# A four-layer network on one core: masked exponents in the state-space stage, its batch change rearranged, and three vector steps of the RWKV stage given to GpSimd

## The reference

```
# layer 0, the mix of each token with the one before it
xx   = shifted(x) - x
mix  = tanh((x + xx * maa_x) @ maa_w1.T)          # four low-rank mixes
xf_f = x + xx * (maa_f + delta_f)                 # f = receptance, decay, key, value inputs

# layer 3: 4 heads, state 128, 256 inner channels
z, x, B, C, dt, A, trap, angles = split(u @ W_in)
adt   = min(-softplus(A), -1e-4) * softplus(dt + bias);  ell = cumsum(adt)
theta = cumsum(angles * dt)
K, Q  = rope(rmsnorm(B) + B_bias, theta), rope(rmsnorm(C) + C_bias, theta)
S[i,j]= (Q_i . K_j) * exp(ell_i - ell_j) * step(i, j)      # zero for i < j
y     = (S @ x + D * x) * silu(z);  out = y @ W_out
```

## Time and profile before

| | |
|---|---|
| time, median of 3 | 2929.28 us (2923.33 to 2929.88) |
| profiled execution | 2918.22 us, of it 2916.0 us from the first to the last instruction |
| busy over the span | PE 2353.3, DVE 2163.2, ACT 1709.3, POOL 1020.3 us |
| granted TensorE clock, mean | 0.893 of full speed |
| RWKV pre stage | 44 to 334 us |
| state-space stage | 2573 to 2916 us, 8 batches |

### The profile page before, as it was taken

The page is one execution under the profiler, slowest core; times in us unless marked ns, Lnnn a source line. Parts: engine busy times, 40 slices in busy tenths (PEclk is TensorE's granted clock), DMA queues, the critical chain, the costliest instruction groups (busy, mean ns, idle before and its releaser), DMA issues. The chain is left out here.

```text
span 2916.0 us, 36851 instructions
## 1 busy us (share of the span) xinstructions
PE 2353.3 (81%) x10377; PEld 1041.9 (36%) x10472; DVE 2163.2 (74%) x5969; ACT 1709.3 (59%) x3093; POOL 1020.3 (35%) x987
## 2 busy tenths in 40 slices
PE   7666378786778999769999989778878888768887
PEld 2211267664343434333333333323331111234443
DVE  6999589995686665556666656587579999567777
ACT  4444344543655666562222278646579999677775
POOL 0222488994244555240000044200020000048886
PEclk8777666767889999989999999989889999889999
DMA  3112575625175765431111033200031111011110
GB/s 132 58 58 73 128 137 108 111 42 148 54 225 109 141 120 109 108 138 48 34 35 37 24 82 91 60 0 0 17 109 45 45 42 43 16 42 33 40 37 26
DMA packets 297801, 211.63 MB, mean 73 GB/s; under 512 B 157640, under 2 KB 262008, under 8 KB 296952
## 3 DMA queue, kind: packets, MB, share of 16 engines
q1 hardware_dynamic: 258992, 189.71, 24.6%
q0 software_dynamic: 20352, 17.05, 4.0%
q10 hardware_dynamic: 18256, 2.52, 0.5%
HBM read 136.18 MB, written 62.52 MB: 68 GB/s over the span
## 5 line engine op out<-in xcount | busy, mean ns | idle before, releaser
L3171 ACT ACTIVATE ca_pw<-ca_ps,ca_mx 128x512 f32<-128x512 f32 x512 | 342.7, 938 | 7.3 <-DVE ca_mx L3207 7.3
L3207 DVE TENSOR_REDUCE ca_mx<-ca_ps 128x1 f32<-128x512 f32 x512 | 311.2, 675 | 0.7 <-PE ca_ps L3138 0.7
L3004 DVE CUSTOM_DVE_ANT_0 mx_sums<-mx_ps,w_w2f 128x384 f32<-128x384 f32 (+3 forms) x512 | 218.0, 486 | 112.2 <-PE mx_ps L2959 110.7
L2947 PE MATMUL gm_ps<-gm_h,w_w2f 128*128 128x512 f32 x512 | 239.0, 607 | 3.1 <-DVE gm_h L3032 3.1
L3171 ACT ACTIVATION_READ_ACCUMULATOR ca_pw<-ca_ps,ca_mx 128x1 f32 x512 | 234.3, 458 | 0.0
L3138 PE MATMUL ca_ps<-qs,ks 128*128 128x512 bf16 x484 | 172.6, 397 | 60.3 <-ACT ca_pw L3171 41.0
L2646 ACT ACTIVATE ta_pw<-ta_ps,w_cst 128x1280 f32<-128x1280 f32 x128 | 168.1, 1322 | 36.2 <-PE ta_ps L2526 36.1
L3076 ACT ACTIVATE gm_h<-gm_ps,w_w2f 128x512 f32<-128x512 f32 x64 | 44.0, 687 | 218.4 <-PE gm_ps L2947 218.4
L2372 ACT ACTIVATE at_pw<-at_ps 128x1280 f32<-128x1280 f32 x128 | 157.1, 1238 | 20.8 <-PE at_ps L2339 20.8
L2778 DVE TENSOR_TENSOR ta_pw<-ta_pw,w_cst 128x384 f32<-128x384 f32 x128 | 70.7, 552 | 132.6 <-ACT ta_pw L2646 128.6
L2691 POOL DMA_INDIRECT Acc<-XN,f_idx x64 | 104.6, 1635 | 153.8 <-DVE XN L2749 139.1
(11 more groups left out here) (574 smaller groups left out, 6202.1 us busy)
## 6 DMA issues: line engine op xcount, KB each, us to landing
Pd<-s_p SPq DMA_DIRECT2D x48, 384.0 KB, 4.6
ex_w<-e_w SPq DMA_DIRECT2D x48, 256.0 KB
Qd<-rp_q SPq DMA_DIRECT2D x4, 2048.0 KB, 11.6
ss_ellb<-Rd SPq DMA_DIRECT2D x32, 256.0 KB, 3.3
qs<-Pd SPq DMA_DIRECT2D x32, 192.0 KB, 4.1
ks<-Pd SPq DMA_DIRECT2D x32, 192.0 KB, 4.5
Pd<-cs_p SPq DMA_DIRECT2D x16, 384.0 KB, 2.4
GX<-Qd SPq DMA_DIRECT2D x44, 128.0 KB
```

The lines of the kernel that those rows point to most:

```text
L2947: last = pe.matmul(at, W(("h1", "h2")[layer])[:, j * 512 + f * 128:j * 512 + (f + 1) * 128], (h0, h1)[layer][:, j, :], start=(j == 0), sto ...
L3004: return v.tensor_tensor_reduce(out=sums[:, bank, at:at + n], in0=ps[:, bank, at:at + n], in1=K["w2f"]("down")[:, T - n:T], scale=-1.0, sc ...
L3171: act.activation(pw[:, h % BUF, jk, :], ps[:, (h * NB + jk) % BANKS, :], ACT.Exp, bias=mx[:, h % H, jk:jk + 1], accum_out=z[:, h % H, jk:j ...
L3207: v.tensor_reduce(mx[:, h % H, jk:jk + 1], ps[:, q % BANKS, :], AX.X, ALU.max, negate=True).then_inc(S["top"], 1)
```

## The change

Three groups of edits.

State-space stage. (1) The decays of a diagonal block get their mask within the exponent: POOL's new `fallen` adds a constant block `later` (0 for a query not before the key, -1e30 otherwise) to ell, where DVE took the minimum before; `low` has a tile for each head now. (2) POOL's `steps` has two instructions a head: strict mask times (gamma - beta dt), a column that the rows stage now makes in COL[:, 0], and plus beta dt; the wait for `clamp` is gone. (3) The order at the change of batch: PE projects the first gate before keys and queries, spreads head 0 before `out`, and the dx products and the next batch's angle projection come between spread(1) and products(0); ACT does Sin, Abs and Sin between the gates and ahead of Ln and Exp, and its dummy Exp is gone; DVE makes bc first and rot after it under a semaphore of its own, `finish` comes behind prepare(0) and its addition at the end of the batch, `add_angles` comes before weigh(0), `one_turn` before weigh(3).

RWKV pre stage. (4) `differences` (without L147, which stays on DVE) and the fourth addition of L169 (the value input) are POOL's; the additions on DVE are three a lane. POOL makes the differences of the next iteration right behind the value inputs of this one. PE's value product and ACT's first Sigmoid wait for the new semaphore xv.

```diff
@@ rwkv_pre_phase, vector
-            def differences(i, a):
+            def shifted(i, a):
                 x = halves(i, a)
-                v.wait_ge(S["xf"][a], i)
-                v.tensor_tensor(xp[:, a, M:T], x[:, 0], x[:, 1], ALU.subtract)
-                v.tensor_tensor(xp[:, a, 1:M], x[:, 1, 0:M - 1], x[:, 0, 1:M], ALU.subtract)
-                v.tensor_scalar(xp[:, a, 0:1], XN[...], -1.0, None, ALU.mult).then_inc(S["diff"][a], 1)
                 v.wait_ge(S["diff"][a], i + 1)
...
-                    for f in range(4):
+                    for f in range(3):
                         last = v.tensor_tensor(split(xf[:, a, f, :]), split(t[:, a, f, :]), x, ALU.add)
@@ rwkv_pre_phase, gpsimd
+            def values_in(i, a):
+                t = buffers(i)[0]
+                g.wait_ge(S["f1"][a], 2 * i + 1)
+                g.wait_ge(S["vps"][a], i)
+                g.tensor_tensor(split(xf[:, a, 3, :]), split(t[:, a, 3, :]), halves(i, a), ALU.add).then_inc(S["xv"][a], 1)
+            for a in range(LANES):
+                differences(0, a)
             for i in range(IT):
+                for a in range(LANES):
+                    values_in(i, a)
+                if i + 1 < IT:
+                    for a in range(LANES):
+                        g.wait_ge(S["xxx"][a], i + 1)
+                        differences(i + 1, a)
@@ l2_gelu_and_rows_phase, vector
-            v.tensor_copy(COL[:, 0:3], cps[:]).then_inc(P["col"], 1)
+            v.tensor_copy(COL[:, 1:3], cps[:, 1:3]).then_inc(P["col"], 1)
...
+            v.tensor_tensor(COL[:, 0], COL[:, 1], COL[:, 2], ALU.subtract).then_inc(P["col"], 1)
@@ ssm_phase, tensor
+            def first_gate(i):
                 pe.wait_ge(S["at"], i + 1)
                 project(i, 7, W("in")[:, 0:128]).then_inc(S["z0"], 1)
+            def second_gate(i):
...
+                spread(0)
+                if i:
+                    out(i - 1)
+                spread(1)
+                pe.wait_ge(S["xt"], i + 1)
+                for n in range(2):
+                    pe.matmul(ps[:, 5 + n, :], dx[...], XN[...], start=True, stop=False, ...)
+                if i + 1 < B:
+                    angles(i + 1)
                 products(0)
...
                 products(3)
                 if i + 1 < B:
+                    first_gate(i + 1)
                     keys_and_queries(i + 1)
-                    gates(i + 1)
+                    second_gate(i + 1)
@@ ssm_phase, scalar
                 gate(i, 0)
+                act.wait_ge(S["clamp"], i + 1)
+                act.activation(th[:, 2, :], th[:, 0, :], ACT.Sin).then_inc(S["sin"], 1)
+                act.activation(th[:, 1, :], th[:, 0, :], ACT.Abs).then_inc(S["abs"], 1)
                 act.wait_ge(S["bcps"], i + 1)
                 act.activation(sq[:], ps[:, 3:5, :], ACT.Square).then_inc(S["sq"], 1)
                 gate(i, 1)
+                act.wait_ge(S["abs"], i + 1)
+                act.activation(th[:, 1, :], th[:, 1, :], ACT.Sin, scale=-1.0, bias=cst("halfpi")).then_inc(S["cos"], 1)
                 act.wait_ge(S["ms"], i + 1)
                 act.activation(sq[:], ps[:, 0:2, :], ACT.Ln, bias=cst("eps")).then_inc(S["std"], 1)
...
-                act.activation(table[:, i:i + 1], cst("eps"), ACT.Exp)
@@ ssm_phase, gpsimd
+            def fallen(i, h):
+                g.wait_ge(HD["ell"][h], 16 * (i + 1))
+                g.wait_ge(HD["dec"][h], i)
+                g.tensor_tensor(low[:, h], ellb[:, h, :].rearrange("p (j x) -> p j x", j=NB),
+                                cst("later").unsqueeze(1).to_broadcast([128, NB, 128]), ALU.add).then_inc(HD["low"][h], 1)
             def steps(i, h):
                 g.wait_ge(HD["dm"][h], i)
+                g.tensor_tensor(mm[:, h], cst("stri")..., COL[:, 0, :, ...]..., ALU.mult).then_inc(HD["m1"][h], 1)
                 g.wait_ge(HD["m1"][h], i + 1)
-                g.tensor_tensor(mm[:, h], mm[:, h], own[:], ALU.add).then_inc(HD["m2"][h], 1)
+                g.tensor_tensor(mm[:, h], mm[:, h], COL[:, 2, :, ...]..., ALU.add).then_inc(HD["m2"][h], 1)
...
-                g.wait_ge(S["clamp"], i + 1)
+                for h in range(H):
+                    fallen(i, h)
+                for h in range(H):
+                    steps(i, h)
@@ ssm_phase, vector
-                    v.tensor_tensor(low[:, h % 2], ellb[:, h, :]..., COL[:, 0, :, ...]..., ALU.min).then_inc(HD["low"][h], 1)
...
                 prepare(0)
-                for h in range(H):
-                    if h + 1 < H:
-                        prepare(h + 1)
-                    elif i + 1 < B:
-                        add_angles(i + 1)
-                    weigh(h)
+                if i:
+                    finish(i - 1)
+                prepare(1)
+                if i + 1 < B:
+                    add_angles(i + 1)
+                weigh(0)
+                prepare(2)
+                weigh(1)
+                prepare(3)
+                weigh(2)
                 if i + 1 < B:
                     one_turn(i + 1)
+                weigh(3)
+                if i + 1 < B:
+                    cosines(i + 1)
+                if i:
+                    add(i - 1)
```

More of the change, by code:

```diff
@@ L150, in _ @@
             for a in range(LANES):
-                differences(0, a)
+                shifted(0, a)
             for i in range(IT):
@@ L3374, in ssm_phase @@
     with Stage(nc, K, at_once=True) as ctx:
-        S = sems(nc, ctx, "ss", "dx bcps ang pj2 xt sq ms std rs norm at th n n1 c1 c2 clamp "
+        S = sems(nc, ctx, "ss", "dx bcps ang pj2 xt sq ms std rs norm rot at th n n1 c1 c2 clamp "
                  "sin abs cos cosm turn yz sps s gx sum stored z0 z0sb z1 z1sb")
@@ L3456, in turn @@
             def turn(i):
-                pe.wait_ge(S["yz"], i)
-                pe.wait_ge(S["z1sb"], i + 1)
-                for j in range(NB):
-                    last = pe.matmul(ps[:, 5 + j // 2, (j % 2) * 256:(j % 2) * 256 + 256],
-                                     XN[:, i * T + j * 128:i * T + (j + 1) * 128],
-                                     W("in")[:, 256:512], start=True, stop=True)
-                last.then_inc(S["pj2"], 1)
-                if i:
-                    out(i - 1)
-                pe.wait_ge(S["norm"], i + 1)
-                pe.wait_ge(S["cosm"], i + 1)
-                pe.wait_ge(S["sin"], i + 1)
                 def spread(h):
@@ L3478, in spread @@
                     last.then_inc(HD["cps"][h], 1)
+                pe.wait_ge(S["yz"], i)
+                for j in range(NB):
+                    last = pe.matmul(ps[:, 5 + j // 2, (j % 2) * 256:(j % 2) * 256 + 256],
+                                     XN[:, i * T + j * 128:i * T + (j + 1) * 128],
+                                     W("in")[:, 256:512], start=True, stop=True)
+                last.then_inc(S["pj2"], 1)
+                pe.wait_ge(S["norm"], i + 1)
+                pe.wait_ge(S["cosm"], i + 1)
+                pe.wait_ge(S["sin"], i + 1)
+                spread(0)
[4 more added lines that the diff above has]
+                for n in range(2):
+                    pe.matmul(ps[:, 5 + n, :], dx[:, n * 128:(n + 1) * 128], XN[:, i * T:(i + 1) * T],
+                              start=True, stop=False, skip_group_check=True)
+                if i + 1 < B:
+                    angles(i + 1)
                 def products(h):
@@ L3502, in outputs @@
                                 last.then_inc(HD["y"][h], 1)
-                spread(0)
-                pe.wait_ge(S["xt"], i + 1)
-                for n in range(2):
-                    pe.matmul(ps[:, 5 + n, :], dx[:, n * 128:(n + 1) * 128], XN[:, i * T:(i + 1) * T],
-                              start=True, stop=False, skip_group_check=True)
-                spread(1)
                 products(0)
@@ L3557, in gates_and_roots @@
                 act.activation(sq[:], sq[:], ACT.Exp, scale=-0.5).then_inc(S["rs"], 1)
-                act.wait_ge(S["clamp"], i + 1)
-                now = th[:]
-                act.activation(now[:, 2, :], now[:, 0, :], ACT.Sin).then_inc(S["sin"], 1)
-                act.activation(now[:, 1, :], now[:, 0, :], ACT.Abs).then_inc(S["abs"], 1)
-                act.wait_ge(S["abs"], i + 1)
-                act.activation(now[:, 1, :], now[:, 1, :], ACT.Sin, scale=-1.0, bias=cst("halfpi")).then_inc(S["cos"], 1)
             def turn(i):
@@ L3593, in turn @@
                         fall = COL[:, 3, jk, i * H + h:i * H + h + 1]
-                        last = act.activation(dec[:, h, at:at + 128], low[:, h % 2, jk, :], ACT.Exp, bias=fall)
+                        last = act.activation(dec[:, h, at:at + 128], low[:, h, jk, :], ACT.Exp, bias=fall)
                         if n > 128:
@@ new lines, in normed, with turned_normed @@
+            def normed(i):
+                v.wait_ge(S["rs"], i + 1)
+                v.wait_ge(HD["b0"][H - 1], i)
+                for n in range(2):
```

(23 more changed lines are left out.)

79 lines of the change are left out of this document (36 added, 43 removed).

## The result

The changed kernel takes 2907.40 us, the median of 4 runs (2905.06 to 2909.94), against 2929.58 us for the kernel before in 4 runs (2923.33 to 2930.88). The ratio is 0.9929, 95% interval 0.9914 to 0.9944: faster by 0.7%. The forecast was 2908 us, a gain of 21 us; the medians lie 22.2 us apart. That the total is right doesn't say that the terms are.

| us | before | after | gained | forecast |
|---|---|---|---|---|
| RWKV pre stage, from the last store of op_tok ahead of it to the first transfer of ex_w behind it | 297.7 | 292.5 | 5.2 | 9 |
| state-space stage, first to last instruction on ss_ps | 336.1 | 322.6 | 13.5 | 12 |
| both | | | 18.7 | 21 |
| layer-1 attention, first to last instruction on ta_ps (untouched) | 349.5 | 359.4 | -9.9 | 0 |
| profiled execution | 2918.22 | 2905.23 | 13.0 | 21 |

What follows compares the result with a forecast made beforehand. DVE, with a PE/ACT chain close behind, was taken to bound the RWKV stage; a cross-engine chain, no full engine, the state-space stage. Gains 9 + 12 = 21 us: 2929.3 - 21 = 2908 us, range 2894 to 2926.

Steps and rivals of the forecast that it cites:

- RWKV, differences: RWKV stage: moving differences to POOL gains 4.0 us in three iterations, 12.0 us; the first differences cost about 1.0 us.
- rival 2: RWKV stage: the shared port eats the gain, differences slow best_eight 1.9 us three times; total 13 us, 2916; chance 0.10.
- RWKV, value inputs: RWKV stage: POOL's addition meets DVE's three at the port, 4 x 0.53 = 2.1 us lost; bound 4 x 1.1 lost.
- lane 0 alone counts: RWKV value additions: only lane 0's 0.53 us delay costs, as DVE had 0.89 us to spare for lane 1.
- State space, change of batch: State-space stage, batch start to end of prepare(0): 2.6 us shorter than 18.95, seven times, 18.2 us gained.
- S: State-space stage: start of a batch, measured at the PE group of keys, queries and first gate.
- Z: State-space stage: end of prepare(0), where the change of batch ends and the heads begin; forecast 16.35 us after batch start.
- no load for Sin behind Silu: ACT at the change of batch: Sin behind Silu supposed to need no table load, so two loads a batch are gone.
- State space, heads: State-space stage after prepare(0): dx and angle projection delay products(0); 0.8 us lost a batch, 5.6 us over seven.
- Rival 1: State-space heads take back the change-of-batch gain, products(0) late by 2.8 us; 7 us faster in all, 2922; chance 0.12.
- first and last batch: State-space stage: first change, where Sin waits for clamp, and last batch together lose 0.4 us.

Runs made afterwards that it cites:

- values_dve: Changed kernel with the value inputs back on DVE (four additions a lane), differences still on POOL: RWKV stage 286.8 us, profiled execution 2899.69 us.
- sines_last: Changed kernel with ACT's Sin, Abs, Sin back behind Ln and Exp and DVE's cosines less 1 behind rot: batch 40.8 us, profiled execution 2928.06 us.
- out_first: Changed kernel with PE's output product of the batch before back ahead of spread(0): batch mostly 41.4 to 41.5 us, profiled execution 2925.54 us.
- the ten kernels under 8: All kernels starting with the changed kernel's new order, each with a 2.75 or 2.76 us PE gap before the first batch's spread(1); nine took 2.87 to 3.68 us.
- best: Changed kernel with POOL's value inputs behind DVE's three additions and, in batch 0 only, POOL's masks waiting for clamp: 2895.67 us, 0.9894 of the kernel before.

## Why the prediction was right, and where not

**RWKV, differences: right.** values_dve has this part alone. Its iterations start 61.12, 64.68 and 64.56 us apart where the kernel before has 65.84, 68.39 and 68.33: 12.2 us gained, forecast 12.0. best_eight of iteration 0 starts 7.06 us behind the last store of op_tok instead of 5.87, so the first differences cost 1.2 us, forecast 1.0. Together 10.9 us (297.7 to 286.8), forecast 11. The search kept its 2.28 us beside POOL, which rival 2 denied.

**RWKV, value inputs: the mechanism right, the term mis-sized.** The forecast was 2.1 us lost, with 4.4 as the bound. The stage with them is 292.5 us, without 286.8: 5.7 us lost, and outside the bound. The 0.53 us for one meeting was about right: three additions take 2.90 us from start to start, forecast 2.95. What failed is "lane 0 alone counts, since [...] DVE had the 0.89 us to spare for lane 1". Lane 1's additions push all that DVE does behind them. They also reach PE: they end at 132.31 in the changed kernel, PE starts lane 1's products (L300) at 132.36, and lane 0's next products stand behind those in PE's program. The wait at the old L188, which was to pay for lane 1, is 0.89, 0, 0.39 and 1.49 us in the changed kernel's four iterations, about what it is without the value inputs on POOL (0.53, 0.33, 0.87 and 1.16 us in values_dve), so it didn't pay. And in lane 1 POOL goes on with the differences, so the additions take 3.40 us, 0.9 us more than four alone. 0.49 + 0.90 us in three iterations and twice 0.49 us in the last make 5.2 of the 5.7 us. The iterations with differences came out 3.0, 2.4 and 3.0 us shorter, where the forecast had 3.5. The sentence of the Trainium skill on the shared interfaces that the prediction quotes (GPSIMD Engine Reference, 1. Specifications) was the right warning, and it had to be applied to every instruction that follows on POOL, not to the one moved.

**State space, change of batch: right.** Exp ends at S + 9.7 (forecast 9.8), spread(0) starts at S + 11.7 (11.8), Z is S + 16.19 (16.35), against 18.95 before: 2.76 us a change, forecast 2.6. The supposition that carried it, no load for Sin behind Silu, holds: three loads a batch. sines_last and out_first show that both moves were needed, 2.8 and 3.5 us a batch, together more than the 2.5 us that the batch gained. With either of them undone alone the gain is gone (stages of 344.0 and 346.6 us against 336.1), since the old kernel held part of each price down by something that the change removed: the dummy Exp, and dx between spread(0) and spread(1). The forecast priced `out` by its 1.88 us, which the one batch of out_first at full clock bears out (1.7 us), and missed that its place also bridges a gap in PE's work.

**State space, heads: over-priced.** Z to the next S is 21.80 us, before 21.58: 0.2 us lost, forecast 0.8. products(0) starts at Z + 4.5 (forecast 5.0), weigh(0) at Z + 6.9 (7.4), half a microsecond better at both. spread(1) ends at Z + 2.1 as forecast; but dx and the angle projection, priced by their durations of 1.88 and 0.91 us, overlap what stands ahead of them and take 1.72 and 0.86 us from start to start, and dx starts 0.16 us before spread(1) ends. Rival 1 had the heads take back everything; they didn't.

**State space, first batch: missed.** The forecast put 0.4 us on first and last batch together. The first lost 4.7 us, for which the port again is the cause in 3.3 us: POOL's masks, freed from their wait for clamp, fell on the five steps of `one_turn`, on which Sin waits. The other 1.4 us fit the clock: dx stood between spread(0) and spread(1) before and left 1.04 us of idle time, now nothing stands there in the first batch, 2.76 us stay, and spread(1) and dx take 1.75 us more than they did (the ten kernels under 8 say the same of spread(1), with one exception). No experiment put dx back; but best, whose clock held behind this gap, has its first y at 51.84 us, 1.8 us ahead of the kernel before. The stretch from the seventh y to the eighth gained 2.9 us instead of 2.5. Summed: 6 x 2.54 + 2.9 - 4.7 = 13.4 us, measured 13.5, forecast 12.

**The sum** came right in part by luck, because errors of both signs met: values 3.6 us and first batch 4.3 us worse than forecast, heads 4.1 us, changes of batch 1.1 us and the last batch 0.4 us better. By stages the gain is 18.7 us; the medians say 22.2 us with a spread of 5 to 8 us in each kernel's runs. Where the other 3 us come from isn't settled; the untouched stages vary by more than that.

## What to carry to other kernels

An offload to POOL is priced by what DVE executes at the same time, and it goes on being priced for everything that POOL does next: ask for each of POOL's instructions which DVE instruction lies beside it. Moving it by one wait, behind DVE's two-input work and beside the search or beside reads of PSUM, was worth 5 us; handing it back was worth as much. When a wait is taken away (clamp), look for what it kept apart, in the first round too, where everything starts at once. And when PE has a gap of some microseconds, an instruction that can stand anywhere belongs in it; look at the first round too, where that instruction may be missing.

## What the runs showed of the hardware

- **DVE beside POOL.** 512-element float32 instructions of DVE on SBUF: L3695 with one tensor input took 0.43 us alone and 1.20 us beside POOL's masks, L3697 with two 0.69 and 1.47 us. The form with one input loses as much as the other (0.77 and 0.78 us). POOL's own addition takes 1.28 us alone and 1.78 us beside DVE's.
- **What isn't slowed.** MAX8 and FIND_INDEX8 took 2.28 to 2.29 us beside POOL's differences and products, and the differences kept their 0.61 us; L158, whose inputs are PSUM and SBUF, took 2.71 to 2.73 us for four with and without POOL.
- **ACT's tables.** Sin behind Silu and Silu behind Sin needed no load in any batch; Sin behind Exp did, 1.28 us, and the Sin started 0.01 us after it.
- **TensorE's clock.** Behind 2.76 us of idle spread(1) took 2.89 to 3.78 us in seven batches of out_first (granted clock 0.63 in the 3 us from the start of the one shown), but 1.99 us in the eighth (1.00) and 1.98 us in the first batch of best; in the first batches of the nine other kernels with this gap it took 2.87 to 3.68 us. Behind 1.04 us it took 1.98 or 1.99 us each time.
